# Gates carried to the slots, and expert rows added to the tokens by the DMA

## The reference

```python
router_logits = x_flat @ w_router
top_vals, top_idx = jax.lax.top_k(router_logits, TOP_K)      # TOP_K = 2
probs = jax.nn.softmax(top_vals, axis=-1)
w_tok = jnp.zeros((N, E)).at[rows, top_idx].add(probs)
h = jnp.square(jax.nn.relu(jnp.einsum('nc,ecd->ned', x_flat, w_fc)))
y = jnp.einsum('ned,edc->nec', h, w_proj)
out = jnp.einsum('nec,ne->nc', y, w_tok)
...
x = _layernorm(x + out)
```

## Time and profile before

| what | value |
|---|---|
| time, three runs | 1543.83 us median (1543.16 to 1544.34) |
| profiled execution, span from the first to the last instruction | 1541.7 us, 26325 instructions |
| PE busy | 1433.5 us, 93% |
| DVE, ACT, POOL busy | 785.6, 724.2 and 377.4 us |
| DMA | 160.10 MB, mean 104 GB/s |
| barrier between residual and expert stage | ends at 1218.4 us |
| ACT's output copies of slot tiles | 39, 598 ns each |
| POOL's first gathers | 16, from 1442.4 to 1462.2 us |
| POOL's second gathers | 16, from 1499.1 to 1527.5 us |

### The profile page before, as it was taken

How to read it: one execution, slowest core, us unless ns; L and a number is a source line. 1 busy time by engine, 2 the same in 40 slices (tenths; PEclk the granted TensorE clock), 3 DMA queues, 4 the chain that set the end, 5 groups by cost and what they waited for, 6 DMA issues and landing times. The chain is left out here.

```text
span 1541.7 us, 26325 instructions
## 1 busy us (share of the span) xinstructions
PE 1433.5 (93%) x8000; PEld 1217.5 (79%) x8001; DVE 785.6 (51%) x1778; ACT 724.2 (47%) x1618; POOL 377.4 (24%) x385
## 2 busy tenths in 40 slices
PE   7999999999999999999999997899999499999770
PEld 5888888888888888888888886688888388888650
DVE  6555555555555655555655654345444333333246
ACT  5655555665655655655655654222222133333223
POOL 1221221212222212222221221321122153344316
PEclk9999999999999999999999999899999699999985
DMA  4111111111011111111111120754454455655516
GB/s 152 55 35 61 44 45 61 34 55 61 27 61 53 35 61 48 41 61 48 41 61 48 41 76 26 263 205 169 172 204 150 166 195 217 241 222 190 163 49 218
DMA packets 63145, 160.10 MB, mean 104 GB/s; under 512 B 7440, under 2 KB 7952, under 8 KB 60688
## 3 DMA queue, kind: packets, MB, share of 16 engines
q1 hardware_dynamic: 55408, 109.46, 21.1%
q0 software_dynamic: 7712, 50.34, 9.1%
HBM read 107.35 MB, written 52.43 MB: 104 GB/s over the span
## 5 line engine op out<-in xcount | busy, mean ns | idle before, releaser
L311 POOL TENSOR_TENSOR small<-small,half 128x4 f32<-128x4 f32 x193 | 194.9, 1010 | 764.5 <-DVE small L340 764.5
L263 ACT ACTIVATE prob<-logit,small 128x128 f32<-128x128 f32 (+3 forms) x256 | 144.1, 563 | 119.5 <-DVE small L412 116.7
L412 DVE CUSTOM_DVE_ANT_0 logit<-score_ps,bias 128x128 f32<-128x128 f32 (+3 forms) x256 | 124.9, 488 | 142.6 <-PE score_ps L505 142.2
L519 PEld LDWEIGHTS y_ps<-vs,prob_t 128*128 128x128 f32 x1280 | 174.7, 191 | 22.6 <-ACT prob_t L270 4.8
L519 PE MATMUL y_ps<-vs,prob_t 128*128 (+1 forms) x1280 | 185.2, 275 | 1.0 <-ACT prob_t L270 0.7
L270 ACT ACTIVATE prob_t<-prob_ps 128x128 f32<-128x128 f32 (+3 forms) x256 | 111.8, 437 | 53.2 <-PE prob_ps L512 52.2
L732 ACT ACTIVATE yt_hi<-turn_ps,subln 128x512 fp32r<-128x512 f32 x64 | 44.0, 688 | 170.4 <-PE turn_ps L960 167.8
L512 PE MATMUL prob_ps<-ident,prob 128*128 128x128 f32 x640 | 112.7, 274 | 3.2 <-ACT prob L263 3.2
L969 PE MATMUL out_ps<-w_hi,yt_hi 128*128 128x512 f32 x256 | 107.4, 419 | 6.4 <-DVE yt_lo L817 6.4
L464 PE MATMUL k_ps<-w_hi,x_hi 128*128 (+1 forms) x256 | 103.5, 404 | 6.0 <-DVE w_lo L372 6.0
L464 PE MATMUL v_ps<-w_hi,x_hi 128*128 (+1 forms) x256 | 106.5, 416 | 0.0
(11 more groups left out here) (177 smaller groups left out, 3255.0 us busy)
## 6 DMA issues: line engine op xcount, KB each, us to landing
y_scratch<-x_now SPq DMA_DIRECT2D x65, 256.0 KB, 2.9
x_raw<-in_x_t SPq DMA_DIRECT2D x64, 256.0 KB, 2.8
y_raw<-y_scratch SPq DMA_DIRECT2D x15, 1024.0 KB
w_raw<-in_w_experts POOLq DMA_DIRECT2D x7, 2048.0 KB, 8.3
w_hi<-in_w_experts POOLq DMA_DIRECT2D x7, 2048.0 KB, 8.5
w_raw<-in_w_all SPq DMA_DIRECT2D x16, 768.0 KB, 5.7
slots_y<-zeros SPq DMA_DIRECT2D x13, 768.0 KB
xs<-slots_x SPq DMA_DIRECT2D x39, 256.0 KB
```

The lines of the kernel that those rows point to most:

```text
L263: nc.scalar.activation(prob[:, 0:width], logit[:, 0:width], ACT.Exp, scale=-1.0, bias=least[:, h:h + 1], accum_out=row_sum[:, (i % 2) * HG ...
L311: nc.gpsimd.tensor_tensor(r, ms, half[:, :], ALU.pow).then_inc(ready, 1)
L412: nc.vector.tensor_tensor_reduce(out=logit[:, 0:width], in0=score_ps[:, 0:width], in1=bias[:, h, T - width:T], scale=1.0, scalar=3e38, op0 ...
L519: mm = nc.tensor.matmul(y_ps[:, h * D:(h + 1) * D], prob_t[:, j * P:(j + 1) * P], one(vs[:, bass.ds(now, 1), j, h * D:(h + 1) * D]), start ...
```

## The change

Each gate is now computed in the residual stage, tile by tile, and scattered to the slots beside x1. ACT takes exp of `gap` (`second_weight`); DVE makes 1/(1+e) and e/(1+e) (`gates`, three 128x1 operations, behind `split_y(0)` in the loop and before the last `layernorm` at the end); POOL scatters one value a token to each of the two slots (`send_gates`, two indirect DMAs into `slots_g`, 4 bytes a row). `slots_g` is cleared once before.

In the expert stage SP loads the 128 gates of a slot tile four tiles ahead, ACT's output copy multiplies by them (`scale=gs`), and there are four output tiles instead of two (the loop runs over four tiles and leaves seven outside). Both gathers add their rows to `x1` in the DMA (`compute_op=ALU.add`), without buffers between; each of the second ones has a semaphore of its own. They start when the tiles up to the end of the seventh and of the eighth expert are stored (`stored_up_to`). DVE's 32 multiply-adds and its gate arithmetic are gone, and the result is normalized in place.

```diff
+            def second_weight(t, b):
+                act.wait_ge(gap_ready, t + 1)
+                act.wait_ge(gates_ready, t + 1)
+                src = gap[:, t:t + 1] if isinstance(t, int) else gap[:, bass.ds(t, 1)]
+                nc.scalar.activation(second[:, b:b + 1], src, ACT.Exp).then_inc(second_ready, 1)
...
+            def send_gates(t, b):
+                pool.wait_ge(gates_ready, t + 3)
+                pool.nop(nofuse=True)
+                for j in range(2):
+                    pool.indirect_dma_start(slots_g, bass.IndirectOffsetOnAxis(ap=slot_now[:, b, j:j + 1], axis=0),
+                                            gate_now[:, b, j:j + 1], None).then_inc(gates_sent[b], 16)
...
                 if not before_step(s, 2):
                     dispatch(s - 2, b)
+                    send_gates(s - 2, b)
...
+            def gates(t, b):
+
+                dve.wait_ge(second_ready, t + 1)
+                nc.vector.tensor_scalar(either[:, :], second[:, b:b + 1], 1.0, None, ALU.add).then_inc(either_ready, 1)
+                dve.wait_ge(either_ready, t + 1)
+                nc.vector.reciprocal(gate_now[:, b, 0:1], either[:, :]).then_inc(first_share, 1)
+                dve.wait_ge(first_share, t + 1)
+                nc.vector.tensor_tensor(gate_now[:, b, 1:2], second[:, b:b + 1], gate_now[:, b, 0:1], ALU.mult)\
+                    .then_inc(gates_ready, 1)
...
+            def load_gates(at, y):
+                sp.dma_start(gs[:, y:y + 1], rows_of(g_slots[bass.ds(at, 1), :, :])).then_inc(g_loaded[y], 16)
...
-                sp.dma_start(out, yo[:, b, :]).then_inc(yo_stored[b], 16)
+                sp.dma_start(out, yo[:, y, :]).then_inc(yo_stored[y], 16)
+                if more(k, 4):
+                    load_gates(at, y)
...
+            def stored_up_to(e):
+
+                end = pool.value_load(end_i[0:1, e:e + 1], min_val=1, max_val=SLOT_TILES)
+                for y in range(YB):
+                    pool.wait_ge(yo_stored[y], (end + (YB - 1 - y)) // YB * 16 + 16)
+                pool.nop(nofuse=True)
+
             pool.wait_ge(slots_known, 1)
...
-                pool.indirect_dma_start(first_rows(t), None, slots_y,
-                                        bass.IndirectOffsetOnAxis(ap=slot_y[:, 0, t:t + 1], axis=0))\
-                    .then_inc(first_gathered, 16)
-            pool.wait_ge(yo_stored[0], 16 * ((SLOT_TILES + 1) // 2 + 1))
-            pool.wait_ge(yo_stored[1], 16 * (SLOT_TILES // 2 + 1))
...
+                pool.indirect_dma_start(x1[:, t, :], None, slots_y,
+                                        bass.IndirectOffsetOnAxis(ap=slot_y[:, 0, t:t + 1], axis=0),
+                                        compute_op=ALU.add).then_inc(first_gathered, 16)
+            stored_up_to(E - 1)
+            pool.wait_ge(first_gathered, 16 * NT)
+            for t in range(NT):
+                pool.indirect_dma_start(x1[:, t, :], None, slots_y,
+                                        bass.IndirectOffsetOnAxis(ap=slot_y[:, 1, t:t + 1], axis=0),
+                                        compute_op=ALU.add).then_inc(second_gathered[t], 16)
...
-                act.wait_ge(yo_stored[b], h * 16 + 16)
-                nc.scalar.activation(yo[:, b, :], ye_ps[b][:, :], ACT.Copy).then_inc(yo_ready, 1)
+                act.wait_ge(yo_stored[y], q * 16 + 16)
+                act.wait_ge(g_loaded[y], q * 16 + 16)
+                nc.scalar.activation(yo[:, y, :], ye_ps[b][:, :], ACT.Copy, scale=gs[:, y:y + 1]).then_inc(yo_ready, 1)
...
             for t in range(NT):
-                add_second(t)
+                dve.wait_ge(second_gathered[t], 16)
+                nc.vector.bn_stats(stats[:, t % 2, :], x1[:, t, :]).then_inc(stats_done, 1)
                 if t >= 1:
                     bias_variance(t - 1)
```

More of the change, by code:

```diff
@@ L645, in residual_phase @@
         slot_f = sb("slot_f", [P, 2])
+        gap = sb("gap", [P, NT])
+        second = sb("second", [P, 2])
+        either = sb("either", [P, 1])
+        gate_now = sb("gate_now", [P, 2, 2])
         def ps(name):
@@ L752, in step @@
                         round_y(g, s * NHG + NHG + g + 1)
+                    if g == 0 and not before_step(s, 2):
+                        second_weight(s - 2, b)
                     if g == 1 and not before_step(s, 1):
@@ L933, in step @@
                 if not before_step(s, 2):
-                    place(s - 2, b)
+                    place(s - 2, b, 32 * h - 32)
                 if turning:
                     split_y(0, s * NHG + NHG + 1)
+                if not before_step(s, 2):
+                    gates(s - 2, b)
                 if not before_step(s, 1):
@@ L1042, in expert_phase @@
         WT = CT + FT
-        gate = sb("gate", [P, 2, NT])
+        gs = sb("gs", [P, YB])
         beyond = sb("beyond", [P, 2 * NT, E - 1])
@@ L1082, in expert_phase @@
         slots_known = sem("slots_known")
-        gap_exp, gates_known = sem("gap_exp"), sem("gates_known")
+        g_loaded = [sem(f"g_loaded{y}") for y in range(YB)]
         we_loaded = sem("we_loaded")
@@ L1089, in expert_phase @@
         down_done, yo_ready = sem("down_done"), sem("yo_ready")
[L1090 to L1093, removed]
+        yo_stored = [sem(f"yo_stored{y}") for y in range(YB)]
+        second_gathered = [sem(f"second_gathered{t}") for t in range(NT)]
+        first_gathered, stats_done = sem("first_gathered"), sem("e_stats_done")
@@ L1100, in expert_phase @@
         out_tiles = out_d.rearrange("(t p) c -> t p c", p=P)
-        LOOPED = (SLOT_TILES - 4) // 2
+        LOOPED = (SLOT_TILES - 4) // YB
         def slot_steps(engine, slot_step):
[L1106 to L1110, removed]
+            with engine.Fori(0, LOOPED) as quad:
+                for y in range(YB):
+                    slot_step(quad * YB + y, y % 2, quad * 2 + y // 2, y, quad)
+            for k in range(YB * LOOPED, SLOT_TILES):
+                slot_step(k, k % 2, k // 2, k % YB, k // YB)
@@ L1112, in more @@
         def more(k, ahead):
-            return (k if isinstance(k, int) else 2 * LOOPED - 1) + ahead < SLOT_TILES
+            return (k if isinstance(k, int) else YB * LOOPED - 1) + ahead < SLOT_TILES
         @block.sync
         def _(sp):
[L1118 to L1124, removed]
+            for y in range(YB):
+                sp.nop(nofuse=True).then_inc(yo_stored[y], 16)
@@ L1141, in _, with slot_step @@
                         pad(sp, e)
-            def slot_step(k, b, h):
+            for b in range(2):
+                sp.wait_ge(gates_sent[b], 32 * (NT // 2))
+            for k in range(YB):
+                load_gates(tile_at(k), k)
+            def slot_step(k, b, h, y, q):
                 if more(k, 4):
-                    start = load(k + 4, b)
+                    at = tile_at(k + 4)
                 if more(k, 4):
@@ L1206, in gather @@
[L1206 to L1211, removed]
-            for t in range(GB - 1):
-                gather(t)
+                pool.indirect_dma_start(x1[:, t, :], None, slots_y,
+                                        bass.IndirectOffsetOnAxis(ap=slot_y[:, 0, t:t + 1], axis=0),
+                                        compute_op=ALU.add).then_inc(first_gathered, 16)
@@ L1229, in _ @@
             act.nop(nofuse=True).then_inc(hid_ready, 1)
-            nc.scalar.activation(gate[:, 1, :], gap[:, :], ACT.Exp).then_inc(gap_exp, 1)
             def round_x(b, count):
@@ L1292, in _ @@
                 .then_inc(slots_known, 1)
-            nc.vector.tensor_tensor(lower[:, 0, :], by_rank[:, :, 0], by_rank[:, :, 1], ALU.is_lt)
-            then(nc.vector.tensor_tensor(lower[:, 1, :], by_rank[:, :, 0], by_rank[:, :, 1], ALU.is_gt))
-            dve.wait_ge(gap_exp, 1)
-            then(nc.vector.tensor_scalar(gap[:, :], gate[:, 1, :], 1.0, None, ALU.add))
-            then(nc.vector.reciprocal(gate[:, 0, :], gap[:, :]))
-            then(nc.vector.tensor_tensor(gate[:, 1, :], gate[:, 1, :], gate[:, 0, :], ALU.mult))
-            for j in range(2):
-                nc.vector.tensor_tensor(part[:, j, 0, :], gate[:, 0, :], lower[:, j, :], ALU.mult)
-                op = nc.vector.tensor_tensor(part[:, j, 1, :], gate[:, 1, :], lower[:, 1 - j, :], ALU.mult)
-            then(op)
-            nc.vector.tensor_tensor(gate[:, :, :], part[:, :, 0, :], part[:, :, 1, :], ALU.add).then_inc(gates_known, 1)
             def split_x(b, count):
```

128 lines of the change are left out of this document (58 added, 70 removed).

## The result

The changed kernel takes 1530.79 us (median of 4 runs, 1529.39 to 1532.13) against 1544.09 (1543.16 to 1545.0): a ratio of 0.9911, with a 95% interval from 0.99 to 0.9923. It is 13.3 us faster, where 7.5 were forecast (1536.3 us); the time lies in the range. The profiled execution has a span of 1528.0 us, 13.7 less than before. But the likeliest case isn't what happened: PE isn't held at all, and that the time still lies this near the forecast is luck (see the part on the prediction).

A forecast was written before the change was run, and what follows sets the result against it. PE was taken to bound the kernel until the last slot tile, held late during gathers; 1504.3 + 3.1 (barrier) + 4.5 (slower gathers) + 22.3 (end) = 1534.2 us span, plus 2.1 gives 1536.3 us; range 1511 to 1553.

The forecast's parts named there:

- the likeliest case: Both gather runs hold PE's completions, adding gathers 1.4 us apart, second run starting early: 1536.3 us, chance 0.42.
- if this run holds PE's completions as the first did: Second gathers, expert stage's end: PE's completions come 22.7 + a after their first issue, at 1504.3 before shifts.
- the two gaps: Sign of being right: two gaps in ACT's output copies, one in each run of gathers, each ending with its run.
- The third rival: No gather run holds PE, so 13.9 us go: 1513.0 us, chance 0.2.
- its second reason: Third rival's alternative to the output buffers having been the wait: adding gathers don't hold PE.
- The second rival: Only the first gather run holds PE; POOL's issue then binds the end: 1529.2 us, chance 0.16.
- The pace x: Time per gather in a run: 1.26 us before, 1.4 taken for adding gathers, upper bound 1.75 if DMA-bound.
- the rival "DMA-bound": Adding gathers bound by the DMA engines, x = 1.75, both runs holding PE: 1547.5 us, chance 0.22.
- Barrier: Last token tile and barrier into the expert stage: +3.1 us from gates and two gate scatters, bounds 0.5 to 5.
- Expert loop: Slot-tile loop: output scaling, gate loads and dropped gate arithmetic together cost 0; four output buffers also 0.
- Second gathers start early: Largest term: they follow tile 35's store, starting at about 1481.6 instead of 1499.07.
- DVE's tile at the end: Final stage: without the add, a token tile costs DVE 0.95 us, fifteen of them 14.3 us.

The follow-up runs named there:

- the paced ones: The kernel before with one useless 128x2 power on POOL ahead of each plain first gather, which then start 1.94 us apart; 1529.49 us.

## Why the prediction was right and where it failed

- **Faster, and inside the range: right. The likeliest case: wrong.** The step that failed is "if this run holds PE's completions as the first did". The reading of the trace of before was right: the gap comes with plain gathers, whatever the buffers (four alone: 1544.14 us) and the loop, and came back with them (1535.39 us; the forecast's sum for a changed kernel whose runs hold PE is 1531.8 at their pace, x = 1.26). But the step took for granted that an adding gather does the same. It doesn't: POOL issues it every 1.85 us, and plain gathers as far apart don't hold PE either. Of the signs of being right the two gaps failed to appear. The third rival, no run holds PE, is what happened; adding gathers that don't hold it stood there as its second reason, with a chance of 0.2.
- **The number was luck.** Two errors went opposite ways: the holds that were forecast didn't come, and the gathers' chain at the end was longer than forecast. The second rival's 1529.2, the nearest number (its terms add up to 1529.1), is luck too: it had the end right, with POOL's issue as the bound and the first power done at 1510.1 (it is at 1511.9), but it got there with a hold in the first run and a faster pace.
- **The third rival's time, 1513.0, was 16.7 us short of the profiled run's 1529.7.** The second run started at 1481.83 instead of 1470.8: 11.0 us, because the first run lasts until 1477 and the second waits for all of its rows. It took 29.3 us to the end of its last issue instead of 22.4: 6.9. The 10.6 us from there to the last bn_stats were forecast as 11.5, and behind that 8.0 (6.3 and the 1.7 around the span) as 8.3.
- **The pace x**: 1.4 was taken, 1.75 the upper bound; it is 1.85, and outside both. The bound came from the DMA engines; what rose is POOL's own issue, 0.95 to 1.54 us, which no row of before could show. The Trainium skill's page "Collectives: The Full Stack", section "Why ReduceScatter is half of AllGather", has an add 1.93 times slower than a copy. The trace agrees about, for the engines: the estimate is 1.8 times. In the 20 us from 1449 there are 10.8 gathers of 262 KB, 2.8 of 4.0 MB; the other 1.2 MB are some 4 us at the rate of the earlier trace rows, and 1.03 x 20 - 4 = 16.6 us of all engines are 1.5 us a gather against 0.87. It isn't what decides, because POOL is slower still; the rival "DMA-bound", with PE held, didn't come, although the engines were full.
- **Barrier**: +3.1 forecast, upper bound 5; it is 6.3 up to ACT's first rounding. Two issues, 2.6, were right. Missed were 2.0 us more from POOL's last scatter to the barrier's end (6.5 against 4.4, put at nothing) and most of the 1.4 us ahead of the last x1: the additions of token tiles 1 to 14 in the residual loop stand 14.42 us apart instead of 14.35 (1004.0 to 1191.5 us, before 1003.8 to 1190.3), about 1 us in all, where 0 was forecast with 4 as the bound. All eight traces with the gates in the loop have 14.41 to 14.43, all six without 14.35 to 14.39. PE shows no wait in the loop, so why a step is longer stays open.
- **Expert loop**: 0 forecast, -1.6 us measured over 32 tiles, 0.05 a tile. The loop over four tiles alone doesn't do it (6.46 us a tile with four buffers alone), and it is gone with the last gates behind the barrier (6.44); why stays open.
- **Second gathers start early**: right: at 1481.83 instead of 1499.07, and 9.2 us of time are lost when it is undone, 1.9 of them ahead of the gathers. What they wait for isn't tile 35's store but the landing of the first run. **DVE's tile at the end**: 0.95 forecast, 0.88 measured (1.76 us for two).

What the change really did: its adding gathers took away a hold of 13.5 us by being slow to issue, which one attribute does alone (1528.96 us). The rest of it, gates, barrier, early start and DVE's shorter end, comes to nothing (+4.7 us up to tile 32 and -5.0 at the end), since 32 gathers of 1.85 us and the powers behind them make POOL the bound of the end.

## What to carry to other kernels

Where an engine's signals come late while a run of indirect DMAs is on, change the pace of the run before anything else: a useless 0.7 us operation between the gathers was worth 16 us here. A DMA that computes was charged twice here, on the DMA engines (1.5 us a gather instead of 0.87, an estimate) and on the engine that issues it (1.54 us instead of 0.95); ask which of the two sets its pace. And put short operations that others wait for between the issues of a long run, not behind it (7.6 us).

## What the runs showed of the hardware

- Plain gathers of 262 KB issued every 1.25 us keep PE's completions from the engines that wait for them: two output copies lie 16 to 20 us apart, in both runs of the kernel with plain gathers. At 1.33 us it is in part so, at 1.85 and 1.94 us not at all.
- It isn't the whole run. In the kernel before, the copy 2.8 us behind the first issue is on time (1445.13); ACT's rounding of this turn of PE is 2.2 us late; and the hold ends 2.8 us after the last issue (1465.04 against 1462.22):

```profile
1448.08 0.60 PE L1375 MATMUL xt_ps<-ident,xs 128*128 128x128 f32 x4
...
1450.92 0.60 ACT L1234 ACTIVATE xt_hi<-xt_ps 128x512 fp32r<-128x512 f32 x1 [2.05 <-remote]
```

- It doesn't go with the DMA engines' load: PE was held at 0.73 to 0.80 and free at 1.03. It doesn't go with the bytes of all transfers either: PE was held at 213 GB/s, by the second run of plain gathers in the changed kernel (first line), and free at 218, with the paced ones (second line). What tells the cases apart is the pace of the gathers. Whether their number or their own bytes count was not tried, as all had 128 rows of 2 KB; why they should delay PE's signals stays open.

```profile
1500.00:1510.00 10.00, 0.66 (x4) 0.42 (x4) 0.21 (x1) 0.69 (x1) 7.56 (x9) 0.70 0.73 213
1448.00:1468.00 20.00, 20.00 (x101) 16.35 (x100) 5.99 (x9) 6.53 (x12) 17.96 (x22) 1.00 0.71 218
```

- An indirect gather that adds takes POOL 1.54 us to issue instead of 0.95, from the first of a run on.
- Small scatters (128 rows of 4 bytes) take POOL nearly as long to issue as rows of 2 KB (0.96 us in the mean of 32, against 1.02).
